# Attention steps of a graph kernel placed in twos on TensorE: two heads' scores, eight transposes, two head pairs' value products

## The reference, cut to what matters

```python
h = relu(layernorm(x)); x = x + L0(h, ...)      # typed graph convolution, 625 nodes, 512 wide
h = relu(layernorm(x)); x = x + L1(h, ...)      # graph attention, 8 heads of 64

def L1(x, edge_index, W_qkv, b_qkv, W_ff, b_ff):
    Q, K, V = split(x @ W_qkv.T + b_qkv)        # each (625, 8, 64)
    scores = einsum('ehd,ehd->eh', Q[receivers], K[senders]) * scale
    ex = exp(scores - segment_max(scores, receivers)[receivers])
    att = ex / segment_sum(ex, receivers)[receivers]
    msg = segment_sum(att[:, :, None] * V[senders], receivers)
    return msg.reshape(n, 512) @ W_ff.T + b_ff
```

## Time and profile before

| | us |
|---|---|
| median of 3 runs | 321.08 |
| lowest and highest | 320.94 to 321.26 |
| the profiled execution | 321.26 |
| its span, first to last instruction | 319.5 |
| attention, from the first score to the last sum | 218.6 to 316.8 |

### The profile page before, as it was taken

One profiled execution on the slowest core, in us unless ns is written; L12 is line 12 of the kernel. 1 busy time (PEld: TensorE's weight loads), 2 busy tenths in 40 slices (PEclk: granted clock), 3 DMA queues, 4 the chain that ended last, 5 costly groups with the idle time before them and its releaser, 6 DMA issues.

```text
span 319.5 us, 5460 instructions
## 1 busy us (share of the span) xinstructions
PE 294.4 (92%) x2006; PEld 226.4 (71%) x2006; DVE 194.0 (61%) x471; ACT 142.9 (45%) x282; POOL 69.8 (22%) x97
## 2 busy tenths in 40 slices
PE   2848699999999999998999999997999999999994
PEld 1513345544677788687887889997888898888882
DVE  5899977986234344334359744967857565565721
ACT  1152234523325322533343505687876464665621
POOL 6045003210655044800012402310002020020202
PEclk9999999999999999999999999999999999999999
DMA  5753992111080300045300000000000000000000
GB/s 181 251 209 131 331 386 106 67 36 55 17 291 8 133 2 2 2 131 139 125 0 0 2 0 3 0 3 0 2 0 2 36 0 35 1 2 35 1 35 29
DMA packets 10970, 22.29 MB, mean 70 GB/s; under 512 B 950, under 2 KB 966, under 8 KB 10938
## 3 DMA queue, kind: packets, MB, share of 16 engines
q1 hardware_dynamic: 8772, 16.80, 15.3%
q0 software_dynamic: 800, 2.62, 2.2%
q10 hardware_dynamic: 1366, 2.45, 2.1%
HBM read 15.60 MB, written 6.26 MB: 68 GB/s over the span
## 4 chain that ended last, share of the span: by engine, by line
PE 81%; DVE 12%; ACT 3%; issue 2%; DMA 1%; DVEq 0%; POOL 0%
PE banks L1239 15%; PE banks L1185 9%; PE banks L1225 9%; PE banks L1325 8%; PE banks L1130 8%; PE banks L1311 7%; PE banks L1300 7%; PE banks L1083 5%; PE banks L1345 5%; DVE key_hot L820 3%; DVE row_hot L827 2%; PE banks L1215 2%; PE banks L1335 2%; PE banks L1172 1%; PE banks L1202 1%
## 5 line engine op out<-in xcount | busy, mean ns | idle before, releaser
L1003 DVE CUSTOM_DVE_ANT_0 s_sb<-banks,mask_add 128x640 f32<-128x640 f32 x40 | 32.6, 822 | 22.2 <-PE banks L1300 22.1
L1083 PE MATMUL banks<-key_hot,row_hot 128*128 128x480 f16 x120 | 32.5, 419 | 9.0 <-DVE key_hot L820 9.0
L660 ACT ACTIVATE p_sb<-s_sb,neg_max 128x640 f32<-128x640 f32 x40 | 32.9, 823 | 17.3 <-DVE neg_max L1003 17.3
L820 DVE TENSOR_SCALAR key_hot<-iota,picked 128x480 f16<-128x480 f16 x120 | 36.9, 374 | 0.0
L1185 PE MATMUL banks<-adjT,h 128*128 128x320 f16 x240 | 33.1, 299 | 0.4 <-DVE zT_even L879 0.4
L1083 PEld LDWEIGHTS banks<-key_hot,row_hot 128*128 128x128 f16 x120 | 12.6, 105 | 26.4 <-DVE key_hot L820 9.2
L1185 PEld LDWEIGHTS banks<-adjT,h 128*128 128x128 f16 x240 | 23.3, 98 | 9.8 <-DVE zT_even L879 0.7
L1311 PE MATMUL banks<-ident,p_sb 128*128 128x128 f32 x200 | 29.6, 275 | 0.2 <-ACT pT L667 0.2
L490 POOL TENSOR_TENSOR msgT<-msg_f,msgT 128x128 fp32r<-128x128 f32 x20 | 8.6, 458 | 95.7 <-ACT msgT L681 95.7
L1239 PE MATMUL banks<-w_hl,zT_even 128*128 128x512 f32 x120 | 29.2, 394 | 0.0
L1300 PE MATMUL banks<-k_hi,q_st 128*128 128x320 f32 x80 | 27.1, 348 | 2.0 <-DVE neg_max L1003 2.0
(11 more groups left out here) (176 smaller groups left out, 466.4 us busy)
## 6 DMA issues: line engine op xcount, KB each, us to landing
w_self<-in_L_gnn_W_self_dram SPq DMA_DIRECT2D x3, 1024.0 KB, 9.4
raw<-in_L_gnn_W_rel_dram SPq DMA_DIRECT2D x3, 1024.0 KB, 15.6
raw<-in_L_gnn_W_qkv_dram SPq DMA_DIRECT2D x3, 1024.0 KB, 5.3
sorted_rows<-zero_rows ACTq DMA_DIRECT2D x1, 1792.0 KB, 10.7
self_rows<-hs SPq DMA_DIRECT2D x7, 256.0 KB, 2.0
hs<-sorted_rows SPq DMA_DIRECT2D x1, 1280.0 KB, 7.2
xs<-in_x_dram SPq DMA_DIRECT2D x1, 1024.0 KB
raw<-in_L_gnn_W_ff_dram SPq DMA_DIRECT2D x1, 1024.0 KB
```

What stands on the lines that cost most here:

```text
L660: nc.scalar.activation(p_sb[:, n % NPR, :], s_sb[:, n % NS, :], ACT.Exp, scale=-1.0, bias=neg_max[:, it, h:h + 1], accum_out=denom[:, it, ...
L820: return nc.vector.tensor_scalar(to_key, iota[:], float(KEYS * w), key, ALU.add, ALU.is_equal)
L1003: nc.vector.tensor_tensor_reduce(s_sb[:, n % NS, :].rearrange("p (a j) -> p a j", a=2), banks[:, c:c + 2, 0:HALF], mask_add[:, it, :].rear ...
L1083: mm(banks[:, w % 2, 0:KEYS], row_hot[:, w % 2, k, :], key_hot[:, w % 2, k, :], start=(k == 0), stop=True, skip_group_check=True).then_inc ...
```

## The change

The due times of three kinds of step are set in twos. Scores (with their smax) of heads 2m and 2m+1 both get the time 2m. Turns and fills 2g and 2g+1 both get the time of turn 2g+1. The products pv 2m and 2m+1 both get the time of pv 2m+1. Exp, norm, rb, msg, ff and out keep their times. No instruction is added or taken away; only their order on PE, DVE and ACT changes, and no buffer changes.

```diff
         for n in range(NT * H):
-            placed += [(n, "score", n), (n + 0.1, "smax", n), (n + 0.7, "exp", n)]
+            placed += [(n // 2 * 2, "score", n), (n // 2 * 2 + 0.1, "smax", n), (n + 0.7, "exp", n)]
         turn_at = [TURN + 4 * f / NT for f in range(NT * NT * H // 4)]
-        for f, at in enumerate(turn_at):
+        for f in range(len(turn_at)):
+            at = turn_at[min(f | 1, len(turn_at) - 1)]
             placed += [(at, "turn", f), (at + 0.1, "fill", f)]
         pv_at = [turn_at[((2 * n + 2) * NT - 1) // 4] + PV for n in range(NT * KD)]
-        placed += [(at, "pv", n) for n, at in enumerate(pv_at)]
+        placed += [(pv_at[n // 2 * 2 + 1], "pv", n) for n in range(NT * KD)]
```

## The result

| | before | with the change |
|---|---|---|
| median, us | 321.16 (4 runs, 320.94 to 321.26) | 323.18 (4 runs, 323.04 to 323.27) |
| profiled execution | 321.26 | 323.23 |
| its span | 319.5 | 321.5 |
| mean granted clock of TensorE | 1.000 | 0.995 |

The ratio is 1.0058, with a 95% interval of 1.0043 to 1.0072: slower, outside the stated range of 319.2 to 322.8.

The account below looks back on a forecast made before the run. PE was taken to bound the attention. Start +1.05, three tiles -3 x 0.73, last stretch -1.56 and four new waits +4 x 0.70 gave +0.10 us: 321.2 us forecast, range 319.2 to 322.8.

Parts of the forecast that it names:

- What bounds the kernel, and that only pv, rb and ff can gain: PE in the attention never waits from about 226 us; alternating scores with turns costs nothing, 1.03 against 1.01 us.
- A tile without new waits: PE from one rb to the next: 18.01 us after the change, 0.73 us less for each of three tiles.
- The second pv of a pair: On PE, a pv directly behind another pv adds 1.04 us, where a single one costs 1.24.
- rival B: Pairs of pv on PE don't pay: each costs 2 x 1.24, nine pairs 1.8 us more, 323.0 us; chance 0.13.
- The ff behind a score: On PE, two ff taken as 1.47 us; 0.09 less a tile if the first weight load hides under the score.
- The new wait: PE waits at turns 14, 24, 34, 44 for ACT's fill behind msg pieces and an exp: 0.70 us, four times.
- The last stretch: PE from rb 3 to rb 4: 15.44 us in place of 17.0, 1.56 us less, before any new wait.
- the block of four ff steps: On PE between rb 3 and rb 4, four ff steps together take 2.75 us.
- The start: First heads up to rb 0: score 5 ahead of turn 0 delays the chain, costing 0.95 to 1.1 us.
- A: PE's wait for ACT's fill doesn't come, or hardly: the sum loses 2.8, 318.4 us; chance 0.17.
- C: Second scores of pairs on PE show waits for their maxima: up to +1.4 us, 322.6 us; chance 0.10.
- the place named as the likeliest surprise: The start of the attention, where an unplaced wait was most likely, all three engines being close behind each other.

Follow-up runs that it names:

- the fills first: Changed kernel with the even fills due 0.01 earlier, so ahead of the exps on ACT: 320.31 us, ratio 0.9957.
- the clock held: Changed kernel with eight more 512-column matmuls on PE behind score 3, results unread: 321.96 us, ratio 1.0018.

## Why the prediction was wrong, step by step

- *What bounds the kernel, and that only pv, rb and ff can gain.* Right: scores in twos moved a tile by 0.06 us, products in twos by 0.72.
- *A tile without new waits, 18.01 us.* Right: 18.07 with the fills first. (Products alone give 18.02, in another order.) The second pv of a pair was mis-sized, 1.10 in place of 1.04 (2.33 to 2.34 a pair against 2.28, nine pairs, 0.5 us). The one row it rested on, at the very end, was a little too cheap (2.35 us for x40 there, 2.40 here); about a quarter of rival B's 0.20 was true. The ff behind a score took the cheaper value that I had kept for the range: 249.64 to 251.03 is 1.39.
- *The new wait, 0.70 us in four tiles.* Right: 0.69 by the starts, and 2.9 us came back when it was taken away. Even so a tile came out 0.07 us longer than forecast: the pairs of pv cost 0.11 more, the ff behind a score 0.08 less, and the rest is in the turns.
- *The last stretch.* Mis-sized by 0.26 us: two pairs of pv, 0.11; the block of four ff steps, 2.83 in place of 2.75; the rest in turns, 0.83 in place of 0.79 ahead of that block.
- *The start, "0.95 to 1.1 us".* **This step failed.** Its chain was right: with the clock up rb 0 came within these bounds. But I carried every duration over from a trace in which the clock never fell, and took the granted clock of 1.00 as a property of the kernel. The row that should have warned me is the 1.34 us idle time in the earlier trace rows: the step that the change moves, turn 0, was the work that kept this gap short. Making it longer cost 1.48 us that no row of before could show, and the bound of 0.3 us on the start left no room for it. With it the start took 2.53 us in place of 1.05.
- *The rivals.* A didn't come: ACT took the fill in its order. B came in part, C didn't (a tile moved by -0.06 us with the scores alone in twos). None of them had the clock, so the place named as the likeliest surprise was right and the mechanism wasn't there.

Without the clock the difference would have been 0.10 + 0.46 (pairs of pv and the small terms), 321.7 us, in the range and near the 321.96 measured with the clock held.

## What to carry to other kernels

When a change moves a step on TensorE, look at whether that step stands in a gap: the granted clock may fall behind the longer gap, and the cost is then more than the wait. Price each kind of step by its neighbours from the trace, and put two of a kind together only where going over to that kind and back costs something; here one line of the three gave all the gain. Where due times set an order, look for ties: 0.01 in a due time was worth 2.9 us.

## What the runs showed of the hardware

In the profiled executions of this kernel an idle gap of 1.34 us, shortly after one of 0.61, left the clock at 1.00, and one of 1.80 us in the same place was followed by the lower level for some three us. The mean clock of every execution agrees in the main: 0.995 or less in 31 of 36 with the longer gap, in 5 of 66 of the kernel before. Eight matmuls whose results nobody reads, in that gap, were worth 1.2 us. Going in and out of the 64-column products costs 0.14 us for each pair that is put together, beside up to 0.17 for the turn ahead.
